# Folding the kept rows of a three-layer CIN block to one column per sample by DMA, with the weighing split between ScalarE and VectorE

## The reference

```
for i, f in enumerate(CIN_LAYERS):            # [128, 128, 128]
    h = prev.shape[1]
    Wr = Ws[i].reshape(h, M, f)
    z = jax.nn.relu(jnp.einsum('bhk,bmk,hmf->bfk', prev, x0, Wr) + bs[i][None, :, None])
    half = f // 2
    results.append(z[:, :half])
    prev = z[:, half:]
pooled = jnp.sum(jnp.concatenate(results, axis=1), axis=-1)
return pooled @ W_lin
```

## Time and profile before

| | |
|---|---|
| time, median of 3 runs (lowest, highest) | 1967.69 us (1966.97, 1968.11) |
| time of the profiled execution | 1967.74 us |
| its span, first to last instruction | 1965.8 us |
| granted clock of TensorE | 1.0 throughout |
| PE busy | 1960.1 us, 100% of the span |
| DVE busy | 1870.5 us, 95% |
| ACT busy | 668.0 us, 34% |
| POOL busy | 156.6 us, 8% |
| DMA engines, mean share of 16, SP's queue and POOL's | 68.0% and 7.7% |

### The profile page before, as it was taken

One profiled execution on the slowest core, in us unless ns is written; L12 is line 12 of the kernel. 1 busy time (PEld: TensorE's weight loads), 2 busy tenths in 40 slices (PEclk: granted clock), 3 DMA queues, 4 the chain that ended last, 5 costly groups with the idle time before them and its releaser, 6 DMA issues.

```text
span 1965.8 us, 30145 instructions
## 1 busy us (share of the span) xinstructions
PE 1960.1 (100%) x10304; PEld 740.1 (38%) x10304; DVE 1870.5 (95%) x1413; ACT 668.0 (34%) x844; POOL 156.6 (8%) x186
## 2 busy tenths in 40 slices
PE   9999999999999999999999999999999999999999
PEld 3333343333333334333343333333333333333333
DVE  8989999999999999999999999999999999999988
ACT  2333234432244422444223443234432244422332
POOL 1001000010100000001001010010100100000000
DMA  7998887778877779767798677987778977778620
GB/s 165 191 193 172 188 176 161 155 165 175 189 160 153 168 160 198 170 143 171 154 201 174 146 165 158 193 179 154 159 158 181 192 149 164 158 167 198 144 43 1
DMA packets 123037, 319.07 MB, mean 162 GB/s; under 512 B 25042, under 2 KB 43883, under 8 KB 123014
## 3 DMA queue, kind: packets, MB, share of 16 engines
q1 hardware_dynamic: 98051, 294.66, 68.0%
q0 software_dynamic: 24192, 23.87, 7.7%
q10 hardware_dynamic: 770, 0.23, 0.1%
HBM read 294.72 MB, written 0.01 MB: 150 GB/s over the span
## 4 chain that ended last, share of the span: by engine, by line
PE 97%; DVE 1%; DMA 0%; ACT 0%; issue 0%; ACTq 0%; DVEq 0%
PE acc L851 37%; PE acc L730 23%; PE acc L926 20%; PE acc L856 11%; PE acc L915 2%; PE acc L722 2%; PE acc L797 1%; DVE prod L420 1%; PE acc L940 1%; PE acc L933 1%; DMA bias<-b 0%; ACT prev L1058 0%; PE acc L737 0%; DVE prod L422 0%; ACTq L1160 0%
## 5 line engine op out<-in xcount | busy, mean ns | idle before, releaser
L420 DVE TENSOR_TENSOR prod<-prev,x_bc 128x2048 f32<-128x2048 f32 x511 | 1141.9, 2283 | 31.7 <-PE acc L933 16.1
L851 PE MATMUL acc<-prod,w_sb 128*64 128x512 f32 x3360 | 746.2, 593 | 0.0
L926 PE MATMUL acc<-prod,w_sb 128*64 128x512 f32 x1064 | 462.1, 593 | 0.0
L851 PEld LDWEIGHTS acc<-prod,w_sb 128*64 128x64 f32 x3360 | 238.7, 137 | 438.8 <-issue 414.3
L933 PE MATMUL acc<-prod,w_sb 128*64 128x512 f32 x840 | 383.9, 593 | 0.0
L730 PE MATMUL acc<-x_rot,w_sb 128*64 128x512 f32 x1240 | 277.5, 593 | 0.0
L1105 ACT ACTIVATE diff<-acc 64x256 f32<-64x256 f32 x56 | 21.2, 379 | 714.9 <-PE acc L856 714.6
L422 DVE TENSOR_TENSOR prod<-prev,x_bc 128x1024 f32<-128x1024 f32 x193 | 229.9, 1218 | 15.9 <-ACT prev L1014 10.1
L926 PEld LDWEIGHTS acc<-prod,w_sb 128*64 128x64 f32 x1064 | 143.9, 137 | 248.2 <-issue 193.3
L393 DVE TENSOR_TENSOR x_rot<-x_rot,x_rep 128x1024 f32<-128x1024 f32 (+1 forms) x186 | 213.9, 1218 | 1.3 <-issue 0.3
L856 PE MATMUL acc<-prod,w_sb 128*64 128x256 f32 x896 | 191.5, 379 | 0.0
(11 more groups left out here) (98 smaller groups left out, 1090.5 us busy)
## 6 DMA issues: line engine op xcount, KB each, us to landing
x_bc<-x SPq DMA_DIRECT2D x312, 256.0 KB, 13.0
x_bc<-x SPq DMA_DIRECT2D x124, 512.0 KB, 19.6
x_rot<-x SPq DMA_DIRECT2D x155, 312.0 KB
x_rot<-x SPq DMA_DIRECT2D x217, 156.0 KB
x_bc<-x SPq DMA_DIRECT2D x124, 128.0 KB, 8.5
x_rep<-x SPq DMA_DIRECT2D x62, 192.0 KB
x_t<-x SPq DMA_DIRECT2D x64, 128.0 KB, 9.0
x_bc<-x_bc POOLq DMA_DIRECT2D x56, 128.0 KB, 10.2
```

The lines of the kernel that those rows point to most:

```text
L420: mul = nc.vector.tensor_tensor(prod[:, s:s + w, :], twice, x_bc[:, u, t:t + w, :], ALU.mult)
L851: mm = nc.tensor.matmul(acc1[f, h, :], w[:, f], prod[:, s, BANK * h:BANK * h + BANK], start=False, stop=stop, skip_group_check=closed)
L926: nc.tensor.matmul(acc2[0:HALF, u, :], w, prod[:, s, 0:BANK], start=(pos == 1), stop=False)
```

## The change

The DMA folds go on until one column per sample is left: four folds for `res01` (1024 to 64 columns) and three for `res2` (512 to 64), in place of two each. The folds of the two tensors are issued in turns, so that a step of the one is under way while the other is waited for. No channel sum is left in the loop. ACT multiplies the folded `res01` of block i-1 by its weights and stores it in `pool`, in `evacuate0(i+1)` between `spread` and `keep01`. DVE multiplies the folded `res2` of block i-2 and adds it to `pool` with one instruction (`weigh_folded2`), behind the fifth of the twelve layer-2 runs of block i. The folds of `res01` now also wait for `pooled01`, that is for ACT's weighing of the block before. The additions of `x_bc` tiles of block i+1 are issued among the folds of block i, in place of ahead of those of block i+1. The semaphores `sum01_ready` and `sum2_ready` are replaced by `pooled01` and `pooled2` where buffers are given back. The blocks outside the loop still sum on DVE at full width. TensorE's and SP's programs do the same work in the same order.

```diff
-                    channel_sum2(i - 2, folded=i * 32 - 32)
                     products0(i + 1)
-                    channel_sum01(i - 1, 1 - u, folded=i * 32 - 32)
-                    products2(i, u, i * (2 * CH) + CH)
+                    products2(i, u, i * (2 * CH) + CH, range(5))
+                    weigh_folded2(i - 2, i * (16 * FOLDS2) - 16 * FOLDS2)
+                    products2(i, u, i * (2 * CH) + CH, range(5, NR))
...
+            def weigh_folded2(i, folded):
+
+                dve.wait_ge(folded2, folded)
+                dve.wait_ge(pooled01, i + 2)
+                column = pool[:, bass.ds(i * BB, BB)]
+                nc.vector.scalar_tensor_tensor(column, res2[:, 0:BB], wl_col[:, 1:2], column, ALU.mult,
+                                               ALU.add).then_inc(pooled2, 1)
...
+            def fold(res, cols, m, folded, done):
+
+                n = cols >> m + 1
+                if m > 0:
+                    pool.wait_ge(folded, done + 16 * m)
                 pool.sem_inc(adds_asked, 1)
+                pool.dma_start(res[:, 0:n], res[:, n:2 * n], accum_op=ALU.add).then_inc(folded, 16)
...
+            def block_adds(i, u, loaded=None):
+
+                done01, done2 = i * (16 * FOLDS01) - 32 * FOLDS01, i * (16 * FOLDS2) - 32 * FOLDS2
+                pool.wait_ge(res01_ready, i * 2 + 1)
+                pool.wait_ge(pooled01, i)
+                fold(res01[1 - u], NB, 0, folded01, done01)
+                fold(res01[1 - u], NB, 1, folded01, done01)
+                pool.wait_ge(res2_ready, i + 1)
+                fold(res2, BANK, 0, folded2, done2)
+                fold(res01[1 - u], NB, 2, folded01, done01)
+                fold(res2, BANK, 1, folded2, done2)
+                if loaded is not None:
+                    add_tile(1 - u, 0, loaded)
+                fold(res01[1 - u], NB, 3, folded01, done01)
+                fold(res2, BANK, 2, folded2, done2)
+                if loaded is not None:
+                    for n in range(1, len(PAIR_TILES)):
+                        add_tile(1 - u, n, loaded)
...
+            def weigh_folded01(i, a, folded):
+
+                act.wait_ge(folded01, folded)
+                nc.scalar.activation(pool[:, bass.ds(i * BB, BB)], res01[a][:, 0:BB], ACT.Copy,
+                                     scale=wl_col[:, 0:1]).then_inc(pooled01, 1)
+
+            def evacuate0(i, a, folded=None):
                 act.wait_ge(acc0_full, i + 1)
                 spread(prev[0], acc0[:, a, :, :], 0, a)
-                act.wait_ge(sum01_ready, i + 1)
+                if folded is not None:
+                    weigh_folded01(i - 2, a, folded)
+                act.wait_ge(pooled01, i)
                 keep01(acc0[:, a, :, :], 0, a)
...
-                act.wait_ge(sum2_ready, i + 1)
+                act.wait_ge(pooled2, i + 1)
                 nc.scalar.activation(res2[:], acc2[:, u, :], ACT.Relu, bias=bias[:, 2:3]).then_inc(res2_ready, 1)
```

More of the change, by code:

```diff
@@ L69, in cin_kernel @@
     SLOT2_REST = [(2 * CH + pos) % RING for pos in range(CH)]
+    FOLDS01, FOLDS2 = (NB // BB).bit_length() - 1, (BANK // BB).bit_length() - 1
     assert NH == 2 and 2 * CH % RING == 0 and NBLK % U == 0 and HALF == 2 * QUAD and M == QPT * T + 3
@@ L399, in product0_made, with products0 @@
                 product0(ON_CHIP[n], rot[0:rows, :, :].rearrange("p h n -> p (h n)"), rows)
-            def products0(i):
+            def products0(i, part=range(C0)):
                 dve.wait_ge(rep_loaded, i * (16 * 3) + 16)
                 for g, (c0, c1) in enumerate(X0_GROUPS):
+                    if c0 not in part:
+                        continue
                     dve.wait_ge(rot_loaded[g], i * (16 * ROT_LOADS[g]))
@@ L543, in channel_sum, with channel_sum01, channel_sum2 @@
             def channel_sum(total, res):
-                return nc.vector.tensor_reduce(total[:], res.rearrange("p (k b) -> p b k", b=BB),
+                return nc.vector.tensor_reduce(total[:], res[:].rearrange("p (k b) -> p b k", b=BB),
                                                mybir.AxisListType.X, ALU.add)
[L548 to L553, removed]
+            def channel_sum01(i, a, n):
+                dve.wait_ge(res01_ready, i * 2 + 3)
                 dve.wait_ge(pooled01, i + 1)
-                channel_sum(sum01, res01[a][:, 0:NB if folded is None else QTR]).then_inc(sum01_ready, 1)
-                dve.wait_ge(sum01_ready, i + 3)
+                channel_sum(sum01, res01[a]).then_inc(sum01_ready, 1)
+                dve.wait_ge(sum01_ready, n)
                 nc.vector.tensor_scalar(pool[:, bass.ds(i * BB, BB)], sum01[:], wl_col[:, 0:1], None,
                                         ALU.mult).then_inc(pooled01, 1)
[L560 to L565, removed]
+            def weigh_folded2(i, folded):
[4 more added lines that the diff above has]
+                                               ALU.add).then_inc(pooled2, 1)
+            def channel_sum2(i, n):
+                dve.wait_ge(res2_ready, i + 3)
                 dve.wait_ge(pooled2, i + 1)
-                channel_sum(sum2, res2[:, 0:BANK if folded is None else P]).then_inc(sum2_ready, 1)
-                dve.wait_ge(sum2_ready, i + 2)
+                channel_sum(sum2, res2).then_inc(sum2_ready, 1)
+                dve.wait_ge(sum2_ready, n)
                 dve.wait_ge(pooled01, i + 2)
@@ L614, in _ @@
             nc.vector.tensor_scalar(wl1_all[:], ones[:], wl_col[:, 0:1], None, ALU.mult).then_inc(wl2_ready, 1)
-            channel_sum01(0, 0)
+            channel_sum01(0, 0, 1)
             products2(1, 1, 3 * CH)
@@ L703, in _ @@
             nc.gpsimd.tensor_tensor(w2_diff[:], second, first, ALU.subtract).then_inc(w2_diff_ready, 1)
-            with pool.Fori(1, STEPS - 1) as j:
-                for u in range(U):
[L706 to L712, removed]
+            def block_adds(i, u, loaded=None):
[15 more added lines that the diff above has]
+                        add_tile(1 - u, n, loaded)
+            for n in range(len(PAIR_TILES)):
+                add_tile(0, n, 16 * QPT)
+            with pool.Fori(1, STEPS - 2) as j:
+                for u in range(U):
+                    block_adds(j * U + u, u, j * (16 * QPT) + 16 * QPT)
+            block_adds(LAST - 3, 0, (STEPS - 1) * (16 * QPT))
+            block_adds(LAST - 2, 1)
         @block.tensor
@@ L1061, in evacuate0_first @@
                 act.wait_ge(acc0_full, 1)
-                act.wait_ge(sum01_ready, 1)
                 for h in range(NH):
@@ L1177, in _ @@
                     evacuate1_by_half(i, u, i * (2 * CH) + CH)
-                    evacuate0(i + 1, 1 - u)
+                    evacuate0(i + 1, 1 - u, i * (16 * FOLDS01) - 16 * FOLDS01)
             n = (LAST - 1) * (2 * CH)
@@ L1187, in _ @@
             act.wait_ge(chunk_used, n + 4 * CH + RING)
-            act.wait_ge(sum2_ready, LAST + 1)
+            act.wait_ge(pooled2, LAST + 1)
             nc.scalar.activation(res2[:], acc2[:, 1, :], ACT.Relu, bias=bias[:, 2:3]).then_inc(res2_ready, 1)
```

22 lines of the change are left out of this document (7 added, 15 removed).

## The result

The changed kernel takes 1970.22 us (median of 20 runs, 1969.59 to 1971.02), the kernel before 1967.80 (20 runs, 1966.95 to 1968.42). The ratio is 1.0013, with a 95% interval of 1.0007 to 1.0019: 2.4 us slower, small, but clear of the noise. Forecast were 1967.4 us, in a range of 1965.4 to 1970.0. By the 0.2% that the prediction gives as what a measurement can tell from no change, it is still "the same"; but it is outside the range, and the sign is not the one forecast. So small a loss is worth following because it points to a place that the prediction had passed over.

What follows compares the result with a forecast made beforehand. TensorE at full pace was taken as the bound. From 1967.74 us profiled, VectorE's 36 us saved counted 0 on the path, ScalarE 0, folds 0, possibly -0.3: 1967.4 us, range 1965.4 to 1970.

Steps and rivals of the forecast that it cites:

- The bound: TensorE at full pace bounds every loop step, 121.32 us each; VectorE is behind it, but not by much.
- The weighing of layer 2 (0.284) stays: On VectorE, this 0.284 us instruction remains per block, now with no sum to wait for.
- becomes longer idle time at the ring: VectorE's saved time lengthens its wait for a ring slot, from 1.15 to about 3.7 us per step.
- The 36 us: VectorE time saved by dropped sums, weighing and waits: 1.29 us per block over 28 blocks, none on the path.
- The folds: GpSimd's fold chain starts later, in a busy stretch; 11 us plus 0.87 per step, landing before its deadlines, cost 0.
- The first rival: Folds reach VectorE's `weigh_folded2` late, delaying seven layer-2 runs: slower, 1973 or 2024 us; chance 0.04.
- ScalarE: One added weighing per block between `spread` and the kept write, 0.23 us (0.20 to 0.38), under 6.6 us cover: cost nothing.
- None of the four: Besides 1 and 3: rival 2, ScalarE's kept write late, slower, 0.01; rival 4, fold wait replaces sum, same, 0.92 with forecast.
- Rival 3: VectorE is the true bound, so up to 36 us would be gained: 1932 us; chance 0.03.
- The sign named for being wrong: Loop step off 121.3 by over 0.1 us: longer, with VectorE waiting for `res<-res` or TensorE for VectorE, rival 1; shorter, rival 3.

Runs made afterwards that it cites:

- the second experiment: The changed kernel with VectorE's weighing of layer 2 moved ahead of the layer-2 products: 1980.02 us, ratio 1.0063 to the kernel before.
- the first experiment: The changed kernel with VectorE's weighing of layer 2 moved behind the twelfth and last layer-2 run: 1967.57 us against 1967.60, ratio 0.9999.

## Why the prediction was wrong

**The bound: right, and read too coarsely.** TensorE is the bound, and its pace in the loop is full but for one place. The sentence "So PE at its full pace is the bound from the first step of the loop to the last" was drawn from groups of 48 and of 16 records. The stall of 0.03 us at the end of layer 2 does not show in those; only the list piece by piece has it (0.46 among 0.43). As a stall it is worth 0.5 us in all, which is what moving the left-over product won back, but it says that the lead is zero there. The prediction took the pitch as its argument that VectorE is never late; a full pitch does not show how much lead there is.

**"The weighing of layer 2 (0.284) stays": the step that failed.** The instruction was there already, so it got no term of its own in the sum, and the path was put at "0" for all of VectorE. But the change moves it, from ahead of layer 0 to the middle of layer 2. Before it, ScalarE lets VectorE go 2.97 us after layer 0 opens; behind it, VectorE has no wait in the first block until the last run is due. At 0.2 us (the next instruction starts 923.25 - 923.06 = 0.19 us after it, though it takes 0.28) and 14 steps it is 2.8 to 3.0 us. The prediction asks of the folds where they now start; it did not ask this of the weighing. It did check what happens if the weighing is late because of a fold, but in the second block, from the run that ended at 981.9 us; of the first block, where VectorE has no ring wait, it asked only when the fold lands.

**"becomes longer idle time at the ring", 1.15 to 3.7 us per step: wrong.** The wait at the ring went down from 1.15 to 0.95 us; the saved time went into the wait for ScalarE, 50.6 us against 5.7 before. That wait was in the trace of before too, 0.42 us in front of the first layer-2 product. A lead that is won ahead of such a gate ends at it, which is why 30.6 us less on an engine at 95% gained nothing. No more than 0.04 us per step was there to be gained in any case: that is all that TensorE lost at the last run, as the runs with the left-over product last show (121.28 against 121.32).

**The 36 us: mis-added as busy time.** 0.59 + 0.29 + 0.25 us are instructions, 28 x 1.13 = 31.6 us, and 30.6 were measured. The remaining 0.16 per block are waits for a sum, which were never part of VectorE's busy time. It changes nothing on the path.

**The folds: right in mechanism and in size.** On GpSimd in the changed kernel (start us, us):

```profile
931.08 0.86 POOL L691 DMA_DIRECT2D res<-res  x1 [15.57 <-ACT pool L1062]
944.22 1.78 POOL L691 DMA_DIRECT2D res<-res  x2 [12.28 <-DMA res<-res]
955.18 0.86 POOL L691 DMA_DIRECT2D res<-res  x1 [9.19 <-DMA res<-res]
...
966.67 1.18 POOL L691 DMA_DIRECT2D res<-res  x1
969.09 0.86 POOL L691 DMA_DIRECT2D res<-res  x1 [1.24 <-DMA res<-res]
```

The folds of `res01` start at 931.08, 944.22, 955.18 and 966.67, the third fold of `res2` at 969.09. Those are steps of 13.1, 11.0 and 11.5 us, where 11.9 was priced. With a last one of 5.8, the median landing time of the 32 KB folds below, it is 969.1 + 5.8 = 975, where 977 was forecast. VectorE asks at 982.8. The first rival (fold late at VectorE) did not occur in the changed kernel, and did in the second experiment.

**ScalarE: right.** Its instruction takes 0.348 us, within the bounds of 0.20 and 0.38, though not the 0.23 that I took near the row of one element; it is not on the path, since the first experiment keeps it and loses nothing. The Trainium skill ("ScalarE: Activation LUTs", What ACT_TABLE_LOAD costs) gives, for an instruction with one per-partition pointer operand, 280 ns plus 0.833 ns per column; for 64 columns that is 333 ns, an estimate from that page. The run agrees within 15 ns, so the page was nearer than my row.

**Rivals and range.** None of the four was it. Rival 3 (VectorE is the true bound) had a grain of truth: VectorE does bound TensorE, but at one run per step and behind a gate, where none of the saved work lay. The sign named for being wrong did show, a step more than 0.1 us longer; but the prediction put a longer step with a wait of TensorE for VectorE down to rival 1, and no fold was late here: VectorE has no wait for `res<-res` in the changed kernel. The sign did not tell a late fold from a late instruction. The range took in a loss of up to 2 us as a mishap of the folds, and ended 0.2 us below the median.

## What to carry to other kernels

Where one engine is at its full pace, saving on its feeder gives nothing, but placing one small instruction can cost: look for the point at which the feeder hands over with no lead, and for the wait of the feeder before it, and treat everything between the two as the path. A small instruction is free where another wait of the feeder follows before that point, as in the second block and in the runs with the left-over product last. To find such a point, list the bound engine's chain piece by piece over one period, not in groups, and look for the one piece that is longer by a few hundredths of a us. Then ask of each moved instruction on which side of the gate it stood, and on which it stands now.

## What the runs showed of the hardware

The time from issue to landing of a DMA addition depends here on when it is issued more than on its size. The changed kernel's list of issues (count, KB, median us to landing):

```profile
x_seed<-x_seed POOLq DMA_DIRECT2D x14, 256.0 KB, 12.2
...
res<-res POOLq DMA_DIRECT2D x42, 64.0 KB, 10.3
...
res<-res POOLq DMA_DIRECT2D x42, 32.0 KB, 5.8
```

The same 256 KB took 3.3 us before, in a quiet stretch, and 12.2 when moved behind the start of the loads (the DMA share is 0.97 from 992 to 1005 us of the changed kernel). A quarter of the bytes, 64 KB, still took 10.3 us. The 32 KB folds of `res` took 5.8 in the median; the one at 969.09 us above is issued as the loads run out (share 1.04 from 955 to 966 us, 0.44 from 969 to 975). The Trainium skill says that a DMA's completion lands only after the earlier writes of its DMA engine, across its queues ("DMA: Bandwidth & Descriptors", Queues, rings and completion order); it says so in a paragraph on the queues of SyncE and ScalarE, and these folds are GpSimd's. The numbers fit it; no run here takes the rule apart from mere sharing of the engines' time.

I had not expected that a fully loaded TensorE would show a delay of 0.2 us of its feeder to a hundredth of a us: 0.20 to 0.21 us per step in four kernels (the change, the doubled weighing against it, the kernel before with one instruction more, and the weighing in the first block alone), with equal steps throughout.
